# Issuing the residual sums' stores and the residuals' loads from GpSimd instead of SyncE in a decoder layer's self-attention

## The reference

```python
x = x + attn(layernorm(x))         # 16 heads of 128; q and k RMS-normed per head; no mask
x = x + cross_attn(layernorm(x), ctx)   # 16 heads of 32, keys and values from a 128-wide context
x = x + ffn(layernorm(x))          # silu gate, width 1408, 8 experts' low-rank terms, top 2
```

```python
q, k, v = (einsum('bse,ehd->bshd', xn, w) for w in (wq, wk, wv))
scores  = einsum('bqhd,bkhd->bhqk', rms_norm(q) * q_scale, rms_norm(k) * k_scale)
out     = einsum('bqhd,hde->bqe', einsum('bhqk,bkhd->bqhd', softmax(scores), v), wo)
```

## Time and profile before

| what | value |
| --- | --- |
| median of 3 runs | 2654.82 us (2654.76 to 2655.66) |
| the profiled execution's own time | 2650.35 us |
| its span (first to last instruction) | 2648.3 us |
| PE busy in the span | 2473.2 us |
| PE busy between 100 and 1260 us | 1120.25 of 1160 us |
| q1, the queue that SP fills | 232.07 MB, 37.7% of the 16 engines' span |

### The profile page before, as it was taken

The page is one execution under the profiler, slowest core; times in us unless marked ns, Lnnn a source line. Parts: engine busy times, 40 slices in busy tenths (PEclk is TensorE's granted clock), DMA queues, the critical chain, the costliest instruction groups (busy, mean ns, idle before and its releaser), DMA issues.

```text
span 2648.3 us, 47124 instructions
## 1 busy us (share of the span) xinstructions
PE 2473.2 (93%) x16390; PEld 1331.7 (50%) x16390; DVE 1655.5 (63%) x3781; ACT 1271.5 (48%) x3266; POOL 868.1 (33%) x801
## 2 busy tenths in 40 slices
PE   6999999999999999999769999989989989989998
PEld 3445554555544555444344464464455455455466
DVE  7777756566666657666475565575665665665544
ACT  4555555555555556555335434434434534443423
POOL 3333333333333333333123323323323322423412
PEclk9999999999999999999769999999999999999999
DMA  5777677776766767787220001001001001000000
GB/s 152 159 183 169 141 167 160 153 171 146 168 151 161 161 153 178 177 181 169 82 79 1 16 2 36 16 1 36 16 1 36 12 6 36 3 15 24 7 17 7
DMA packets 454611, 235.18 MB, mean 89 GB/s; under 512 B 388328, under 2 KB 391016, under 8 KB 454376
## 3 DMA queue, kind: packets, MB, share of 16 engines
q1 hardware_dynamic: 454376, 232.07, 37.7%
HBM read 78.66 MB, written 32.77 MB: 42 GB/s over the span
## 4 chain that ended last, share of the span: by engine, by line
PE 79%; DVE 12%; issue 4%; ACT 3%; POOL 1%; DMA 1%; SPq 1%; DVEq 0%; ACTq 0%; POOLq 0%
PE ps L1358 22%; PE ps L1359 21%; PE ps L1360 21%; DVE mem L1192 2%; PE ps L1491 2%; DVE mem L1196 2%; PE ps L1493 2%; PE ps L1492 2%; PE ps L1501 1%; PE ps L1505 1%; PE ps L1503 1%; PE ps L1544 1%; PE ps L1589 1%; PE ps L1563 1%; PE ps L1532 1%
## 5 line engine op out<-in xcount | busy, mean ns | idle before, releaser
L1358 PE MATMUL ps<-mem 128*128 128x512 f16 (+6 forms) x3924 | 1203.1, 326 | 71.4 <-issue 29.4
L1359 PE MATMUL ps<-mem 128*128 128x512 f16 (+6 forms) x3924 | 1216.7, 325 | 0.0
L1360 PE MATMUL ps<-mem 128*128 128x512 f16 (+6 forms) x3924 | 1200.5, 325 | 0.0
L1358 PEld LDWEIGHTS ps<-mem 128*128 128x128 f16 (+3 forms) x3924 | 407.0, 104 | 391.9 <-issue 78.5
L1360 PEld LDWEIGHTS ps<-mem 128*128 128x128 f16 (+3 forms) x3924 | 408.0, 104 | 311.2 <-issue 8.7
L1359 PEld LDWEIGHTS ps<-mem 128*128 128x128 f16 (+3 forms) x3924 | 409.8, 104 | 300.6 <-issue 9.9
L697 POOL TENSOR_TENSOR mem<-mem 128x500 f32<-128x500 f32 (+1 forms) x231 | 269.8, 1168 | 354.6 <-ACT mem L932 197.8
L647 POOL TENSOR_TENSOR mem<-mem 128x8 f32<-128x8 f32 x100 | 163.7, 1637 | 518.6 <-DVE mem L1004 518.6
L793 ACT ACTIVATE mem<-ps,mem 100x100 f32<-100x100 f32 x512 | 169.2, 345 | 224.1 <-DVE mem L1034 223.1
L1314 DVE TENSOR_TENSOR mem<-mem 128x500 f16<-128x500 f32 (+1 forms) x231 | 144.4, 648 | 188.2 <-ACT mem L914 184.4
L711 POOL TENSOR_TENSOR mem<-mem 100x400 f32<-100x400 f32 x128 | 107.7, 853 | 345.7 <-DVE mem L1206 345.7
(11 more groups left out here) (121 smaller groups left out, 3151.7 us busy)
## 6 DMA issues: line engine op xcount, KB each, us to landing
x<-mem SPq DMA_DIRECT2D x100, 256.0 KB, 2.8
mem<-x SPq DMA_DIRECT2D x75, 256.0 KB, 3.4
mem<-in_x SPq DMA_DIRECT2D x50, 256.0 KB, 3.5
mem<-x SPq DMA_DIRECT2D x12, 1000.0 KB
mem<-mem SPq DMA_DIRECT2D x32, 200.0 KB
out<-mem SPq DMA_DIRECT2D x6, 1000.0 KB
mem<-in_wq SPq DMA_DIRECT2D x4, 1024.0 KB, 6.5
mem<-in_wk SPq DMA_DIRECT2D x4, 1024.0 KB, 6.7
```

The source lines that it names most:

```text
L1358: pe.matmul(out_ap, ah, bh, start=(i == 0), stop=False)
L1359: pe.matmul(out_ap, ah, bl, start=False, stop=False)
L1360: mm = pe.matmul(out_ap, al, bh, start=False, stop=(i == len(pairs) - 1))
```

## The change

`store_sum` and `load_residual` move from SP's queue into GpSimd's, word for word, and stand there behind `probs_lo(n + 1)` of the same step. GpSimd's loop runs three steps longer for the last sums. SP gets an explicit wait on the last `mix_values` in front of pieces 13 to 19, GpSimd one on the last three stores in front of the cross-attention.

```diff
@@ sync: the two functions are taken out, and in the loop
-                for w in summed_at(n - 1):
-                    store_sum(w)
-                    if w + 2 < ALL:
-                        load_residual(w + 2)
-                if n == -3:
-                    load_residual(0)
-                    load_residual(1)
@@ sync: behind the loop
+            sp.wait_ge(s["o"], STEPS)
             for n in range(B_IN_A, len(B_PIECES)):
                 load_piece_b(n)
@@ gpsimd
+            def load_residual(w):
+
+                t = w % TILES
+                if w >= 3:
+                    pool.wait_ge(s[f"st{w % 3}"], stored(w - 3))
+                if w >= TILES:
+                    pool.wait_ge(s[f"st{(w - TILES) % 3}"], stored(w - TILES))
+                src = x if w < TILES else x1
+                pool.dma_start(xr[:, w % 3, :], src[t * P:(t + 1) * P, :]).then_inc(s[f"xr{w % 3}"], 16)
+
+            def store_sum(w):
+                t = w % TILES
+                pool.wait_ge(s["add"], w + 1)
+                pool.dma_start(x1[t * P:(t + 1) * P, :], xr[:, w % 3, :]).then_inc(s[f"st{w % 3}"], 16)
+
-            for n in range(FIRST_STEP, STEPS):
+            for n in range(FIRST_STEP, STEPS + 3):
...
                     norm(n + 1)
                     probs_lo(n + 1)
+                for w in summed_at(n - 1):
+                    store_sum(w)
+                    if w + 2 < ALL:
+                        load_residual(w + 2)
+                if n == -3:
+                    load_residual(0)
+                    load_residual(1)
...
+            for w in range(ALL - 3, ALL):
+                pool.wait_ge(s[f"st{w % 3}"], stored(w))
             cross_attention(0, GB, 0)
```

More of the change, by code:

```diff
@@ L510, in load_x @@
                 sp.dma_start(xin[:, u % 3, :], x[u * P:(u + 1) * P, :]).then_inc(s[f"xin{u % 3}"], 16)
[L512 to L525, removed]
             def turn_tile(u):
```

## The result

| | time before | time after | ratio after/before |
| --- | --- | --- | --- |
| median of 4 runs each, us | 2654.79 (2653.13 to 2655.66) | 2707.17 (2700.57 to 2708.78) | 1.0194 [1.0179, 1.021] |

The change makes the kernel 1.9% slower, some 52 us; the forecast was 2653.0, with a range up to 2672. In the changed kernel `turn_tile` is line 522 (537 before), `turn_probs` 541 (556), `rms_power` 626 (647), `norm` 632 (653), the store 660, the load 655, and the first of the three matmuls of a product 1361 (1358).

The account below looks back on a forecast made before the run. PE was taken to bound the self-attention, its pauses before scores waiting for the transpose of q and k. The terms -4 + 4 + 0 + 0 - 1.5 = -1.5 us took the 2654.82 median to 2653, range 2638 to 2672.

Parts of the forecast that it names:

- The bound and the wait: Self-attention: PE sets the time, and its 17 pauses (27.4 us) before scores wait for the transpose of q and k.
- SP's issues removed: SP's queue before `turn_tile`: 1.1 us less issue counts at 4 of 17 pauses, -4 us (bounds 0 and -19).
- The traffic moved in time: Store and load now meet the transposes: 0.4 us on 10 tiles, +4 us; ceiling 1.9 us on 20, +38.
- the floor: Lower bound of the traffic's cost, 0: with the store 2.6 us ahead of `turn_tile`, the first transpose landed in 4.4 us.
- POOL's two issues: POOL before `norm` and `rms_power`: a pair, assumed 2 us, fits into its short waits of 2.29 and 3.42: 0.
- Its overrun: Rival at POOL: a pair above 2.29 us delays `norm`, above 3.42 `rms_power` too; 2669 to 2705 us, chance 0.12.
- DVE holding POOL up: Rival at line 983, group 0: DVE's scaling keeps POOL from preparing transfers, at worst +30 us, 2683; chance 0.04.
- Added waits: POOL's waits on `add` and on a store three sums back: none added, 0.
- residuals in time: DVE's sums: the tightest residual load has 7.5 us for a 3.1 us landing, so 1.5 us later fits: 0.
- The seam: Weight piece at the self-attention's end: starts sooner without the pair ahead, PE's 6.33 us wait shrinks, -1.5 us (bounds 0, -2.9).
- Transposes meet: Rival before scores: the moved pair delays `turn_tile`'s landing; 1.5 us on 15 tiles gives +17, 2672 us; chance 0.14.
- Transposes pass: Rival before scores: with POOL's own queue, transposes no longer stand behind 512 KB; -17, 2638 us; chance 0.25.

Follow-up runs that it names:

- e8: The changed kernel with all of SP's weight pieces, those of the later stages too, issued behind `turn_tile`: 2724.0 us, ratio 1.0275.
- e11: The changed kernel with POOL's store held until `turn_probs` has landed; also called the eleventh kernel: 2760.64 us, ratio 1.0417.
- e4: The kernel before, with the store and load left on SP but issued behind `turn_tile`: 2646.27 us, ratio 0.9978.
- the dummy pair: The kernel before, transfers still on SP, with two unused powers on POOL where the changed kernel issues store and load: ratio 1.0009.
- e2: The changed kernel with POOL issuing store and load earlier, between `norm` and `probs_lo`: 2671.14 us, ratio 1.0067.

## Why the prediction was wrong, point by point

*The bound and the wait were right.* PE's pauses before scores, which wait for `turn_tile`, decide; the loss goes roughly with them wherever no new wait was added (e8 and e11 added one).

*SP's issues removed, -4 us: nowhere to be seen.* What SP saved (1.1 us a step) went into its waits: in `turn_probs` for PE 304.7 us instead of 239.1, for `plo` 106.0 instead of 98.7. And the longer issue of the tile's transposes (+1.0 us at the median) took it back. That the term can be real, the gain of e4 allows, but it isn't measured by itself.

*The traffic moved in time, +4 us: the step that failed.* It put 0.4 us on 10 tiles, "nearer to the floor, whose rows show the same meeting". They did not. In that step before, the load and `turn_probs` went out at

```profile
619.75 0.36 SPq L520 DMA_DIRECT2D mem<-x  x1
620.21 1.26 SPq L556 DMA_TRANSPOSE mem<-mem  x1
```

and so the store 2.6 us and the load 1.9 us ahead of `turn_tile` (621.64 in the earlier trace rows), 1.2 and 0.5 us ahead of `turn_probs`. By the forecast's own figure the 512 KB take 1.9 us, so they were nearly through when the tile's first bytes came; in the two windows from 620 to 622 us 513 KB moved. And this was a tight step: in the next the store stands 4.2 us ahead of `turn_tile`. After the change the store goes out with `turn_probs` and the load behind it, 0.9 us ahead of `turn_tile` (840.71 to 841.60): they share the engines with both. The measured size is 0.8 us on the tile's landing and 1.1 on the probabilities' at the median, and far more where two transposes or a weight piece come together. Nor are only 10 tiles near: the pauses went from 17 to 30 and gained 40 us, ten times the term. The forecast's ceiling was 38. Nor had it a term for the probabilities' transposes, which came later by more than the tile's.

*What the sum left out.* PE's busy time grew by 16 us, of which about 15 by the estimate above stand in stretches at a granted clock of 0.50 behind such pauses (as from 858 to 862). No term of the forecast had it: it counted the pauses only. 36.8 + 16.2 is the whole of the 53 us.

*POOL's two issues, 0: right*, and 1.18 us a pair against the 2 assumed; the dummy pair confirms it. Its overrun needed the wait of the eleventh kernel. *DVE holding POOL up:* the candidate, line 983 (986 now), runs in group 0, and of POOL's 25 loads there the first took 754 ns to issue, the others about 550; all other issues took 544 to 630. So nothing of the 1.2 us each was seen.

*Added waits, residuals in time: right but for crumbs.* POOL waits on `add` for 15.1 us in 4 times, and once, in the stretch above, 1.8 us on an older store; DVE waits twice for a residual, 3.8 us in all. The load lands in 4.5 us from POOL, against 3.4 from SP before (3.1 over loads and stores together in the earlier trace rows); issued from POOL earlier (e2) it took 3.7, which points to the meeting again.

*The seam, -1.5: right, and small.* The same pause of PE (6.33 in the earlier trace rows) is now

```profile
1319.92 0.20 PE L1361 MATMUL ps<-mem 100*128 100x100 f16 x1 [3.97 <-DVE mem L1052]
```

2.4 us less, within the bound of -2.9.

*The rivals.* "Transposes meet" came true, with a median landing right at the mark that the forecast set for it (5.3 where "above 5.3" was asked, 4.9 the limit for no change); its own size, 22.5 - 5.5 us, was a third of what came, for both reasons above. "Transposes pass" is refuted: with the pair in a queue of its own the transposes landed later, not sooner. The Trainium skill bears on this on its page "DMA: Bandwidth & Descriptors" (Issuing engines are not separate DMA queues): transfers from SyncE, ScalarE and GpSimd run on the same 16 engines and interleave, and issuing from several saves only issue time. The table above agrees with the first half, and shows what that interleaving costs here; as to the second, issue time was what SP had to spare here.

*What stays open.* How the engines divide their time between a transpose and plain packets is argued from windows (133 GB/s at a share of 1.22), not measured by itself. What keeps a third of the loss when the pair goes 2.9 us earlier (e2), with the median landings of before, is open, and so is what the larger packets add at the end of the table.

## What to carry to other kernels

When a transfer moves to another queue, compare the moment at which its bytes will run with that of the transfers that somebody waits for, here transposing ones: in these runs the moment of issue, a few microseconds either way, decided most of the loss, and no effect of the issuing engine by itself was seen. A transfer that nobody waits for soon belongs behind the urgent one in the same queue, where the order is fixed; on a second queue it goes whenever that engine comes to it, which here was right behind `probs_lo`, the very moment that released the urgent transfer. And price PE's pauses with what the clock loses behind them.

## What the runs showed of the hardware

- A transposing transfer beside plain ones lands later: 256 KB issued with it cost 0.3 to 0.4 us at the tile's median landing (4.8 and 4.9 against 4.5) and 0.5 to 0.8 at the probabilities'; 512 KB cost 0.8 and 1.1, and with 1 MB of weights ahead the issue of two transposes took 14.1 us instead of 4.6.
- Issues by POOL are short and even (store 0.63 us, load 0.55; SP's took 0.54 and 0.37); the load's landing is slower beside the transposes (4.5 us, from SP before 3.4), and was 3.7 when issued earlier.
- The moved 52.44 MB go in 16000 packets from POOL, the data in 4096 bytes each; from SP they were 28800 (454376 in the queue before, 425576 after), the data in 2048 bytes each.
- The granted clock was 0.50 in stretches at and right behind PE's longer pauses, 12 of them in the changed kernel's self-attention (64.7 us) and 5 before (27.2 us); by the estimate above that took about 15 of the 53 us lost.
